# Running bucket counts in PSUM by half blocks, for a graph network's edge ranks

## What is computed

```python
# relational: messages by source, summed at the destination (edges come sorted by dst)
m = c[:, 0:1] * (h[src] @ bases[0]) + ...           # c = coef[edge_type]
h = relu(segment_sum(m, dst) + h @ loopw + bias) + h_prev
# mean layers: gathered at dst, summed at src
agg = segment_sum(x[dst] * edge_weight[:, None], src)
h = concat([x, agg / deg]) @ W.T + b
x = layernorm(x + h)
```

## Time and profile before

| | |
|---|---|
| median of 3 runs | 7757.05 us (7752.96 to 7761.15) |
| the profiled execution | 7750.85 us, span 7749.0 |
| POOL: gathers L680 | 3276 of 958 ns (layers 1, 2, 4, 5), 819 of 975 ns (layer 0) |
| POOL: scatters L629, gathers L661 | 832 of 969 ns, 832 of 945 ns |
| DVE in `rank` | L1307 265.2 us, L1314 132.3 us, L1300 95.6 us |

### The profile page before, as it was taken

The page is one execution under the profiler, slowest core; times in us unless marked ns, Lnnn a source line. Parts: engine busy times, 40 slices in busy tenths (PEclk is TensorE's granted clock), DMA queues, the critical chain, the costliest instruction groups (busy, mean ns, idle before and its releaser), DMA issues. The chain is left out here.

```text
span 7749.0 us, 133241 instructions
## 1 busy us (share of the span) xinstructions
PE 5240.5 (68%) x25966; PEld 4651.5 (60%) x25967; DVE 3236.1 (42%) x10580; ACT 1009.2 (13%) x2622; POOL 5606.2 (72%) x6200
## 2 busy tenths in 40 slices
PE   6777777777776666667777777667776766544444
PEld 5667666766656555667666766556655655533333
DVE  5454454554555555544444662222223333212222
ACT  1111111111111111122222011111111111100000
POOL 6777767777767777677777337777767777677776
PEclk7777777677777777655555887777677777655555
DMA  3222222222222222222222652222222222212222
GB/s 107 79 78 76 78 75 74 78 78 78 78 55 56 57 58 57 60 66 65 66 65 66 181 148 55 57 59 57 59 54 56 58 57 59 54 53 57 55 56 54
DMA packets 348777, 538.27 MB, mean 69 GB/s; under 512 B 124457, under 2 KB 204823, under 8 KB 347975
## 3 DMA queue, kind: packets, MB, share of 16 engines
q0 software_dynamic: 184416, 378.91, 18.2%
q1 hardware_dynamic: 115315, 127.96, 5.9%
q10 hardware_dynamic: 48500, 26.51, 1.2%
HBM read 448.48 MB, written 80.14 MB: 68 GB/s over the span
## 5 line engine op out<-in xcount | busy, mean ns | idle before, releaser
L680 POOL DMA_INDIRECT ring<-h_table,edges_i x3276 | 3136.8, 958 | 1075.6 <-issue 1032.9
L968 PE MATMUL sum<-onehot,ring 128*128 128x128 f32 x8320 | 1737.9, 346 | 1014.7 <-DMA ring<-h_table,edges_i 802.0
L968 PEld LDWEIGHTS sum<-onehot,ring 128*128 128x128 f32 x8320 | 1399.2, 240 | 1313.5 <-DMA ring<-h_table,edges_i 778.5
L1267 DVE TENSOR_TENSOR acc<-msg,acc 128x16 f32 x4160 | 727.7, 175 | 2682.4 <-PE msg L975 2167.2
L975 PE MATMUL msg<-work,mix_w 128*128 128x128 f32 x4992 | 1032.3, 391 | 278.6 <-ACT work L760 271.7
L975 PEld LDWEIGHTS msg<-work,mix_w 128*128 128x128 f32 x4992 | 954.3, 294 | 352.5 <-issue 332.6
L760 ACT ACTIVATE work<-sum 128x512 f32<-128x512 f32 x1040 | 619.9, 597 | 3719.2 <-PE sum L968 3631.6
L629 POOL DMA_INDIRECT sorted_rows<-ring,pos_i x832 | 805.8, 969 | 283.0 <-issue 245.8
L680 POOL DMA_INDIRECT ring<-in_x_dram,edges_i x819 | 798.8, 975 | 280.8 <-issue 253.9
L661 POOL DMA_INDIRECT ring<-h_table,pos_i x832 | 786.7, 945 | 275.3 <-issue 275.3
L975 PE MATMUL msg<-work,rel_w 128*128 128x128 f32 x3328 | 731.8, 409 | 182.8 <-ACT work L760 181.0
(11 more groups left out here) (197 smaller groups left out, 3628.1 us busy)
## 6 DMA issues: line engine op xcount, KB each, us to landing
lent<-h_table SPq DMA_DIRECT2D x6656, 0.5 KB
ring<-sorted_rows SPq DMA_DIRECT2D x208, 260.0 KB, 3.1
ring<-h_table,edges_i POOLq DMA_INDIRECT x3276
edges_i<-bucket_flat SPq DMA_DIRECT2D x208, 208.0 KB
lent<-in_x_dram SPq DMA_DIRECT2D x1664, 0.5 KB
h_table<-rows ACTq DMA_DIRECT2D x78, 256.0 KB
ring<-h_table SPq DMA_DIRECT2D x832, 8.0 KB
sorted_rows<-ring,pos_i POOLq DMA_INDIRECT x832
```

The source lines that it names most:

```text
L680: nc.gpsimd.indirect_dma_start(out=rows_in[:, s, :], out_offset=None, in_=rows_of[:, :], in_offset=bass.IndirectOffsetOnAxis(ap=srcT_i[:, ...
L968: last = nc.tensor.matmul(SUM[q % 2][:, t * KEYS:(t + 1) * KEYS], rows_in[:, 4 * q + t, :], onehot[:, 4 * q + t, :], start=True, stop=True)
L1267: nc.vector.tensor_tensor(acc[:, at], MSG[h][:, s * WIN:(s + 1) * WIN], acc[:, at], ALU.add).then_inc(added, 1)
```

## The change

The running sum is no longer kept in SBUF. `so_far` is half of the bank `AGG` (104 partitions, 512 columns). Each half block is scanned into it, starting from its own last column, and multiplied by the marks at once; only then may the next half be scanned. So the order on DVE changes from scan, scan, product, product to scan, product, scan, product. The columns in which TensorE leaves the places are the first 8 of the same ones, so the first scan of a turn waits for `pos_kept` of the turn before. `ranked_set`, raised once a turn, becomes `rank_used`, raised by each product: TensorE waits for both products, each scan for the product before it, and the wait for `pos_summed` ahead of the products goes. The clearing of `run` becomes a copy of one zero column, and the total of layer 2 reads `so_far` after a wait for `pos_kept`.

```diff
+        so_far = AGG[0:BUCKETS, 0:BLOCK_EDGES // 2]
...
                     def sum_pos(i):
-                        pe.wait_ge(ranked_set, i + (r * TURNS + 1))
+                        pe.wait_ge(rank_used, i * 2 + (2 * r * TURNS + 3))
                         pe.wait_ge(pos_kept, i + (r * TURNS + 1))
...
+            dve.sem_inc(rank_used, 1)
...
                         dve.wait_ge(rank_step, 4 * TURNS + 1)
+                        dve.wait_ge(pos_kept, 2 * TURNS + 1)
                         nc.vector.tensor_scalar(total[0:BUCKETS, :], ident[0:BUCKETS, 0:BUCKETS],
-                                                run[0:BUCKETS, BLOCK_EDGES - 1:BLOCK_EDGES], None, ALU.mult).then_inc(totals_set, 1)
+                                                so_far[:, BLOCK_EDGES // 2 - 1:BLOCK_EDGES // 2], None, ALU.mult).then_inc(totals_set, 1)
...
-                    nc.vector.memset(run[:, :], 0.0).then_inc(rank_step, 1)
+                    nc.vector.tensor_copy(so_far[:, BLOCK_EDGES // 2 - 1:BLOCK_EDGES // 2], zero[0:BUCKETS, 0:1]).then_inc(rank_step, 1)
...
                     for h in range(2):
+                        part_of = slice(h * half, (h + 1) * half)
                         dve.wait_ge(bucket_used[h], n + 2)
                         dve.wait_ge(rank_step, n * 2 + (h + 1))
-                        hot = bucket_hot[:, h * half:(h + 1) * half]
-                        last = BLOCK_EDGES - 1 if h == 0 else half - 1
-                        nc.vector.tensor_tensor_scan(run[0:BUCKETS, h * half:(h + 1) * half], hot,
+                        dve.wait_ge(rank_used, n * 2 + (h + 1))
+                        if h == 0:
+                            dve.wait_ge(pos_kept, n + 1)
+                        nc.vector.tensor_tensor_scan(so_far, bucket_hot[:, part_of],
                                                      IOTA[0:BUCKETS, KEYS:KEYS + 1].broadcast_to([BUCKETS, half]),
-                                                     run[0:BUCKETS, last:last + 1], ALU.add, ALU.max).then_inc(rank_step, 1)
-                    dve.wait_ge(pos_summed, n + 1)
-                    for h in range(2):
-                        part_of = slice(h * half, (h + 1) * half)
+                                                     so_far[:, half - 1:half], ALU.add, ALU.max).then_inc(rank_step, 1)
                         dve.wait_ge(rank_step, n * 2 + (h + 2))
-                        ins = nc.vector.tensor_tensor(ranked[:, part_of], run[0:BUCKETS, part_of], bucket_hot[:, part_of], ALU.mult)
-                    ins.then_inc(ranked_set, 1)
+                        nc.vector.tensor_tensor(ranked[:, part_of], so_far, bucket_hot[:, part_of], ALU.mult)\
+                           .then_inc(rank_used, 1)
```

More of the change, by code:

```diff
@@ L365, in build @@
         bucket_used = [sem(f"bucket_used{h}") for h in range(2)]
-        rank_step, ranked_set, pos_summed, pos_kept = sem("rank_step"), sem("ranked_set"), sem("pos_summed"), sem("pos_kept")
+        rank_step, rank_used, pos_summed, pos_kept = sem("rank_step"), sem("rank_used"), sem("pos_summed"), sem("pos_kept")
         totals_set, totals_in = sem("totals_set"), sem("totals_in")
```

## The result

| | before | after |
|---|---|---|
| median | 7755.01 us (8 runs) | 7729.88 us (8 runs, 7727.23 to 7736.02) |
| ratio | | 0.9969, 95% interval 0.9958 to 0.9979 |
| the profiled execution | 7750.85, span 7749.0 | 7731.86, span 7730.0 |

7735.5 had been forecast, a gain of 21.5.

The account below looks back on a forecast made before the run. GpSimd's pace between indirect DMAs was taken as the bound. Of 22.4 us of gathers lengthened beside products, 0.9 are lost, the other terms are 0 or covered: 7757.05 - 21.5 = 7735.5 us; 8 in 10 range 7726 to 7753.

Parts of the forecast that it names:

- The bound: GpSimd's pace from one indirect DMA to the next: 5759 x 1.26 = 7256 us of a span of 7749.
- The 22.4 us beside products: Layers 0 and 1: 65 gathers lengthened while a product runs; with its input in PSUM all 22.4 us go.
- 0.9 us lost in the first turns: First four turns: 0.9 us of the gain only lengthens GpSimd's 10.26 us wait before the gather at 125.92.
- Rival 1, nothing moves: The product delays gathers by something that stays, its SBUF output or the traffic around it: 7757 us, chance 0.14.
- What the page says: VectorE instructions with two SBUF inputs contend with GpSimd reading SBUF; with at most one they don't.
- Rival 2, the marks hit more often: The remaining bucket comparisons (L1300) lengthen more gathers, so half the gain comes: 7746 us, chance 0.13.
- The longer step: VectorE's rank step, now three dependent steps instead of one: +0.2 to +0.3 us a turn, covered by idle time.
- The wait for the places: Wait for `pos_kept` ahead of each first scan passes at once, ACT's copy being done 1.53 us earlier at tightest: 0.
- Rival 3, slower: Scan in PSUM far slower, rank step longer by more than VectorE's 8.1 us idle: about 7930 us, chance 0.03.
- The profile's marks: Signs in the profile after: L680's mean in layers 0 and 1 falls from 975 and 976 to about 962.

Follow-up runs that it names:

- The four kernels on one chip: Changed kernel again 7732.44 us; with the running sum back in SBUF 7749.61; with two additional products a turn from two SBUF inputs 7755.86, from one PSUM input 7732.59.
- the short products: The kernel before with each product cut into four of 128 columns, both inputs still in SBUF: 7775.52 us against 7783.69, ratio 0.9988.

## Why the prediction was right, point by point

- *The bound.* Right: POOL's pace from gather to gather is the time. The four kernels on one chip show it: 24 us more in the gathers (16.5 against 40.5) is 24 us more in the span.
- *The 22.4 us beside products.* Right, and it all went. The form of the instruction was read from its neighbours L1255 and L1418 in the earlier trace rows, and the kernel with PSUM and SBUF inputs more (7732.59) shows that reading to hold.
- *0.9 us lost in the first turns.* Right in place and size: the gap grew by 0.7.
- *Rival 1, nothing moves.* Its best argument, 39 products on a gather without effect, has an answer that I missed. In the trace of before, a gather is long beside products only if it *starts* while one runs. If it starts 0.16 us into the pair of products it takes 0.37 longer, at 0.83 it takes 0.30 longer, at 0.03 before the pair or earlier nothing: always what is left of that single product, less 0.13 us. So the earlier trace rows isn't a pair that falls between gathers, as the prediction has it: its gather starts 0.54 us into the pair, when 0.14 of the first product is left. Against products what counts is the start of a gather; I take it for the reading of the 128 row numbers, which no run tested. The rows of 495.10 and 455.09 above fit: 0.58 and 0.60 of the product left, 0.46 and 0.47 longer.
- *What the page says.* The Trainium skill's rule (SBUF — State Buffer, "Who interferes with whom"), two SBUF inputs against a GpSimd instruction that reads SBUF, agrees with all four kernels that vary the inputs. Its added remark, that `tensor_tensor` doesn't stall a DMA from GpSimd's queue, doesn't hold for these gathers: they are held by up to 0.5 us. The prediction told the rule for instructions with at most one SBUF input without its exception: the page leaves out those in a 2-port mode, and names `tensor_scalar` among the operations that can enter one. The marks are a `tensor_scalar`, and the trace shows them lengthening gathers (8.3 us before, 9.1 after). Whether they ran in that mode no row shows.
- *Rival 2, the marks hit more often.* It did not come: 9.1 us instead of 8.3, and 9 to 12 in other profiles.
- *The longer step.* A mis-sized term, without effect: from the first scan's start to the last product's end it takes 4.16 us instead of 3.77 (medians), +0.39 where +0.2 to +0.3 stood. A product behind its scan costs 0.04, but a scan behind a product 0.13, and I had taken both from the scan behind a scan.
- *The wait for the places.* Right: ACT was done at least 1.54 us ahead.
- *Rival 3, slower.* The scan in PSUM is 13 ns longer, not twice as long. That a step longer than its cover costs time is real, but the threshold was too high: 6.5 us, not 8.1. I had read the one turn of the earlier trace rows; the median over the turns, 6.1, which stands in the same prediction, was the better number.
- *The profile's marks.* 962 ns was forecast for the mean of L680 (now L681), 963 measured in both stages. The prediction had also called itself wrong if that mean fell and POOL's idle time for TensorE rose. It rose in layer 0, from 20.6 to 24.1 us, of which 0.7 are the gap named above, and fell in layer 1, from 15.2 to 14.0: 2.3 us in sum against 19.3 saved, too little to undo the gain.

My expectation for the short products was wrong in its size. I took the instructions to fall anywhere on POOL's grid of 1.26 us. They don't: the step's place against the next gathers takes few values, I suppose because it is started by the landing of POOL's own gathers (in before, the gather starts 0.74, 0.42 or 0.03 us ahead of the pair, or 0.13 to 0.16, 0.52, 0.83 or 1.23 us into it). With few values a sum for evenly spread ones is no more than a guess. For the products of before it was near (25 us worked out, 22.4 measured) by luck. A second part of the miss is in no sum of mine: 10 of the 87 gathers that are long beside short products are held not only by the one that they start beside but on through the next, one of them by 0.71 us. That is 3.6 of the 14.5 us; what is left of the product, less 0.13, gives the other 10.9.

## What to carry to other kernels

When GpSimd's indirect DMAs set the pace, look at the length of each against what VectorE runs at its start. Here an instruction with two SBUF inputs, or a `tensor_scalar` from SBUF to SBUF, held the gather until it ended, and the same work with one input in PSUM didn't. The number of such instructions times their mean length is not the cost; the cost is what is left of them when a gather starts, so for one instruction it falls with its length faster than in proportion (22.4 us beside 208 products of 0.68 us, 15 beside 832 of 0.28). And an engine's idle time is a cover with an end: 5 us more work a turn cost next to nothing on VectorE, which idled 6 us in one stretch of the turn, and 10.5 us more cost 4.0 a turn.

## What the runs showed of the hardware

- A VectorE `tensor_tensor` of 0.69 us with both inputs in SBUF held a gather that started 0.09 us behind it by 0.47 us, with its output in SBUF. With the output in PSUM one that started 0.11 us behind it was held by 0.46. With one input in PSUM: 0.96 us, no hold. A gather that started before such a product was not lengthened.
- A `tensor_scalar` from integers in SBUF to SBUF of 0.50 us also holds gathers: making it twice cost 12 to 14 us, replacing it by a form with a PSUM input gave 5 to 10. It lengthened by 0.04 to 0.13 us also 13 gathers that had started before it.
- A `scalar_tensor_tensor` of 0.69 us with two inputs in SBUF (`y` from `acc` and `xT`) held a gather that started 0.05 us behind it by 0.51 us, at 387.67 in the changed kernel.
- A `tensor_tensor` of 104x512 behind a wait took 692 ns with both inputs in SBUF and 691 with one in PSUM; without the wait two in a row take 1.27 us.
- A `tensor_tensor_scan` with its output and its carry in PSUM took 1288 ns, with both in SBUF 1275.
- The gathers of the last stage took 945 ns in the mean in some executions, 956 in others and 948 in one (the short products), each with one pace from start to end of the stage; the executions' times differ by up to 30 us over 5759 indirect DMAs. What chooses the pace is open.
